# The beginning of a fused RWKV attention and mixture-of-experts kernel: decay logarithms earlier, the bonus as two operations over all heads, identity products on TensorE

## What is computed

```python
x = x + attn(layernorm(x))      # 16 heads of 16 channels
x = x + moe(layernorm(x))       # 8 experts, top 2, capacity 320 per batch row
```

```python
Wmat = where(i > j, w ** (i - j - 1), 0) + eye * u     # w = exp(-exp(time_decay))
y    = (r @ k * Wmat) @ v + r @ state * w ** i
out  = (groupnorm(y) * ln_w + ln_b) * gelu(g) @ Wo.T
```

## Time and profile before

| | us |
|---|---|
| median of 3 runs | 866.69 |
| lowest, highest | 865.9, 867.45 |
| the profiled execution | 867.18 |
| its span in the profile | 865.1 |
| TensorE matmuls busy | 826.1 (95% of the span) |
| VectorE busy | 498.3 (58%) |
| ScalarE busy | 490.9 (57%) |
| GpSimd busy | 465.3 (54%) |

### The profile page before, as it was taken

How to read it: one execution, slowest core, us unless ns; L and a number is a source line. 1 busy time by engine, 2 the same in 40 slices (tenths; PEclk the granted TensorE clock), 3 DMA queues, 4 the chain that set the end, 5 groups by cost and what they waited for, 6 DMA issues and landing times. The chain is left out here.

```text
span 865.1 us, 17505 instructions
## 1 busy us (share of the span) xinstructions
PE 826.1 (95%) x6343; PEld 679.8 (79%) x6343; DVE 498.3 (58%) x1237; ACT 490.9 (57%) x876; POOL 465.3 (54%) x497
## 2 busy tenths in 40 slices
PE   3999999999999997999999999999999999999995
PEld 3678878778878776878898787898788888787884
DVE  6888888998888755435442543443543543443441
ACT  4578888888888795445533534543543543552331
POOL 6455477777787765575435455435355443436214
PEclk9999999999999999999999999999999999999998
DMA  4942131113111122754234334334145242404113
GB/s 147 357 174 69 39 129 53 51 51 102 58 50 52 52 85 70 217 138 124 69 49 82 99 73 83 97 69 88 57 104 93 70 97 31 115 2 50 19 13 42
DMA packets 50471, 74.01 MB, mean 86 GB/s; under 512 B 5056, under 2 KB 42176, under 8 KB 50368
## 3 DMA queue, kind: packets, MB, share of 16 engines
q1 hardware_dynamic: 35488, 53.46, 18.9%
q0 software_dynamic: 14592, 19.18, 13.0%
q10 hardware_dynamic: 288, 0.01, 0.0%
HBM read 38.41 MB, written 34.22 MB: 84 GB/s over the span
## 5 line engine op out<-in xcount | busy, mean ns | idle before, releaser
L1584 POOL DMA_INDIRECT out<-ysb,index x80 | 124.7, 1559 | 146.3 <-DVE ysb L1820 110.1
L1933 PE MATMUL p<-xh,whi 128*128 128x512 f32 (+1 forms) x504 | 190.1, 377 | 4.6 <-PEq L1486 4.0
L1797 DVE TENSOR_TENSOR hid<-gated,p 128x512 f32<-128x512 f32 (+1 forms) x126 | 80.9, 642 | 193.9 <-ACT gated L1646 193.9
L1935 PE MATMUL p<-xh,wlo 128*128 128x512 f32 (+1 forms) x504 | 189.9, 377 | 0.0
L1934 PE MATMUL p<-xl,whi 128*128 128x512 f32 (+1 forms) x504 | 189.6, 376 | 0.0
L1646 ACT ACTIVATE gated<-p 128x512 f32<-128x512 f32 (+1 forms) x126 | 70.9, 563 | 174.8 <-PE p L1935 174.8
L1959 PE MATMUL py<-w,hh 128*128 128x512 f32 x448 | 162.4, 403 | 3.7 <-DVE hl L1081 3.0
L1573 POOL TENSOR_TENSOR wlo<-wraw,whi 128x448 fp32r<-128x448 f32 x56 | 71.2, 1274 | 97.8 <-ACT whi L1632 93.7
L1933 PEld LDWEIGHTS p<-xh,whi 128*128 128x128 f32 x504 | 94.7, 188 | 25.7 <-issue 7.4
L1934 PEld LDWEIGHTS p<-xl,whi 128*128 128x128 f32 x504 | 95.0, 188 | 18.7
L1935 PEld LDWEIGHTS p<-xh,wlo 128*128 128x128 f32 x504 | 94.7, 188 | 18.6
(11 more groups left out here) (204 smaller groups left out, 1440.1 us busy)
## 6 DMA issues: line engine op xcount, KB each, us to landing
wraw<-in_w SPq DMA_DIRECT2D x24, 896.0 KB, 5.0
disp<-wraw SPq DMA_DIRECT2D x16, 662.5 KB, 9.2
xtok<-disp SPq DMA_DIRECT2D x16, 530.0 KB, 5.5
x_ring<-in_x SPq DMA_DIRECT2D x16, 256.0 KB, 4.0
out<-x SPq DMA_DIRECT2D x16, 256.0 KB, 2.2
xtok<-disp SPq DMA_DIRECT2D x8, 265.0 KB, 4.0
out<-ysb,index POOLq DMA_INDIRECT x80, 3.8
disp<-row,slot_i POOLq DMA_INDIRECT x64, 2.9
```

What stands on the lines that cost most here:

```text
L1584: nc.gpsimd.indirect_dma_start(out, bass.IndirectOffsetOnAxis(ap=index[e.const % 2][:, t:t + 1], axis=0), ysb[j % NY][:], None, compute_op ...
L1797: nc.vector.tensor_tensor(hid[k][:, 0:w], gated[k][:, 0:w], p3[k][:, 0:w], ALU.mult).then_inc(hid_ready, 1)
L1933: nc.tensor.matmul(dst[:, 0:w], hi[m][:, wcut], xh[xcut], start=(kt == 0), stop=False)
L1935: ins = nc.tensor.matmul(dst[:, 0:w], lo[m][:, wcut], xh[xcut], start=False, stop=(kt == KT - 1))
```

## The change

Four edits, all in the program's beginning:

1. `decay_logs` moves on DVE from iteration c = -1 (behind `mixing(0, 1)`) to iteration c = -3, behind `stats1(0)`. Its exponential on ACT moves from behind `pairs(0)` to behind `turned1(0)`, and `decay_tables` from behind `key(0)` to in front of `receptance(0)`.
2. `stats1(2)` moves on DVE from in front of `mixing(0, 2)` to behind the four masks of step 0.
3. `bonus` becomes two operations over all heads: identity times u into a borrowed tile (`kept.xtok`), and `dmask` plus that tile. The first stands in front of `decayed_k(0)`, the second behind it.
4. PE issues 14 products of the identity with itself in front of `turn1(0)` and 6 behind it. They write into `pY`, which nobody reads before the first `across`, a product that starts a new sum there.

```diff
+BEFORE_TURN, BEHIND_TURN = 14, 6
...
             turned1(c + 1)
+            if c == -1:
+                mask_table()
             group_rstd(c - 1)
...
             normed2(c - 2)
+            if c == -1:
+                decay_tables()
             receptance(c + 1)
             pairs(c + 1)
-            if c == -1:
-                mask_table()
             key(c + 1)
-            if c == -1:
-                decay_tables()
...
+        on_diagonal = kept.xtok[:].rearrange("p t c -> p (t c)")[:, 0:H * Q].rearrange("p (h q) -> p h q", q=Q)
-        def bonus(half):
+        def bonus():
             dve.wait_ge(late_in, 16 * NLATE)
+            chain.link(nc.vector.tensor_tensor(on_diagonal, ident[:].unsqueeze(1).to_broadcast([P, H, Q]),
+                                               u_sb[:].unsqueeze(2).to_broadcast([P, H, Q]), ALU.mult))
+        def add_bonus():
             dve.wait_ge(set_act, 2)
-            for h in range(half * H // 2, (half + 1) * H // 2):
-                ins = nc.vector.scalar_tensor_tensor(dmask[:, h, :], ident[:], u_sb[:, h:h + 1], dmask[:, h, :],
-                                                     ALU.mult, ALU.add)
-            chain.link(ins)
+            chain.link(nc.vector.tensor_tensor(dmask[:], dmask[:], on_diagonal, ALU.add))
...
             if c == -1:
-                decay_logs()
                 head_parity()
...
-            stats1(c + 3)
+            if c != -1:
+                stats1(c + 3)
+            if c == -3:
+                decay_logs()
...
             if c == -1:
-                bonus(0)
+                bonus()
             decayed_k(c + 1)
             if c == -1:
-                bonus(1)
+                add_bonus()
...
             if c == -1:
+                stats1(2)
                 slot_tables()
...
+        def warm(n):
+            for _ in range(n):
+                nc.tensor.matmul(pY[:, 0, 0:P], ident[:], ident[:], start=True, stop=True)
         for c in range(-1, TAIL):
+            if c == -1:
+                warm(BEFORE_TURN)
             scores_a(c)
             across(c, 0)
             turn1(c + 1)
+            if c == -1:
+                warm(BEHIND_TURN)
```

## The result

The change made the kernel slower: 872.72 us (median; 871.91 to 873.47) against 866.96 (865.90 to 867.45), a ratio of 1.0065 [1.0049, 1.0081], 5.8 us. The forecast was 866.1 with a range up to 867.4.

What follows compares the result with a forecast made beforehand. TensorE was taken to bound the kernel, through step 1's first projection. Masks 1.55 us earlier less 1.0 for moved statistics gave 0.55 gained: 866.6 for the profiled execution, 866.1 for the median, range 863.2 to 867.4.

Steps and rivals of the forecast that it cites:

- What bounds the kernel: TensorE has least room, so each edit is measured by the start of step 1's first projection, 30.18 us before.
- Edit 1: Logarithms in VectorE's first pause hold POOL's second norm operation; `shift` comes 1.9 us later (bounds 0 to 2.3).
- Edit 4: Early identity products, hidden in TensorE's waits, may raise its clock, winning 0.43 us at transposes and 1.42 at first projection.
- The sum up to v: Centring of v's weight ends at 17.2 instead of 19.38, so v's projection starts 2.3 us earlier than 19.53.
- Edits 3 and 2: Two-operation bonus worth nothing by itself on VectorE, masks 1.55 us earlier; moved statistics cost 1.0 us behind the masks.
- v to masks: Step 0, from the start of v's projection at 17.2 to the masks' start at 23.8.
- the second rival: POOL's two operations precede the bonus product; step 1's projection at 30.4, 0.2 us late; 867.2, bad case 868; chance 0.15.
- Masks to start: First projection of step 1 comes 5.8 us behind the masks, including 1.0 for the moved statistics.
- The first (no hold): Rival: POOL's first norm isn't held, step 1's first projection at 27.0, gain 3.2 us, 863.5; chance 0.24.
- the 0.08 for slower: Chance of a time above 868.4 us: the second rival's far end and what had not been seen.

Runs made afterwards that it cites:

- e1: The kernel before plus only the 20 identity products (14 ahead of the first transposes, 6 behind); 871.80 us, ratio 1.0055.
- e5: The kernel before plus the 20 identity products cut to one column each, so the array has next to nothing to do; 872.15 us, ratio 1.0056.
- e13: The kernel before plus 80 already fulfilled waits on TensorE spread over iterations 1 to 10, no products; 870.54 us, ratio 1.0043.
- e12: The kernel before plus the 20 identity products and 177 already fulfilled waits spread over TensorE's attention iterations; 868.73 us, ratio 1.0020.
- e15: The whole changed kernel plus 177 already fulfilled waits spread over TensorE's iterations 1 to 12; 866.84 us, ratio 0.9995.
- e6: The kernel before plus seven full identity products ahead of the first transposes and none behind; 869.51 us, ratio 1.0022.
- e10: The kernel of e7 plus four 512-column products, three ahead of the first transposes and one behind; 866.26 us, ratio 0.9989.
- e2: The changed kernel without the identity products, the other three edits kept; 867.33 us, ratio 1.0002.
- e4: The kernel before plus only the early decay logarithms; 866.49 us, ratio 0.9995.
- e7: The kernel before plus the early decay logarithms, with VectorE waiting for step 0's first `rstd` ahead of them; 865.39 us, ratio 0.9979.
- e16: The whole changed kernel plus the 177 spread waits and VectorE's wait for the first `rstd` ahead of the logarithms; 865.26 us, ratio 0.9970.
- e3: The changed kernel with the decay logarithms and their exponentials back in the old places; 870.85 us, ratio 1.0043.
- e14: The kernel of e7 plus the 20 identity products and 177 already fulfilled waits on TensorE; 865.37 us, ratio 0.9978.
- e11: The kernel of e7 plus the bonus as two operations over all heads; 865.21 us, ratio 0.9974.
- e9: The kernel before plus 80 already fulfilled waits at the beginning of TensorE's stream; 875.64 us, ratio 1.0101.

## Why the prediction was wrong

**What bounds the kernel: here is the step that failed.** "The measure of the change is therefore one instant: the start of the first projection of step 1". That the rest of the program stays the same was assumed with it, and the products were priced by their duration alone. But their number moved the expert phase by 79 instructions in TensorE's stream, and 3 to 4 us of pauses came between 440 and 740 us (e1, e5, e13 have them, e12 and e15 have not). The waits of the kernel before had a small sign of it, the 0.6 us at `py` behind a join, but no row that gives the price of moving it; the question to ask was what a longer stream does to the branches behind it. The start itself failed as well: it was forecast at 29.6 and came at 32.55. Of these 3.0 us, 2.2 were the clock (32.55 against e15's 30.37); the rest is the hold at the centring, less what was regained behind it (both below).

The Trainium skill has a rule that I didn't weigh ("Runtime: NRT & Kernel Launch", Instruction fetch mechanics): instructions are fetched in blocks of 256 in sequence, and a taken branch whose target lies outside the fetched window stalls its engine. The runs agree with the size (moved by 79 the pauses come, moved by 256 they go) and with the place (where TensorE leaves the arm of an If). The trace agrees further in that each of the 27 pauses ends 1.2 to 1.7 us behind the end of a 16 KB packet of instructions. What TensorE does in those last 1.2 to 1.7 us no record shows, and packets stand at joins without a pause too, so that this is the mechanism fits well and isn't proven. e6 and e10, moved by 28 and 16 or one less, had one pause, ahead of or among the third join's transposes, and not the one that before has 2 us further on.

**Edit 1: right.** Held 1.9 us: `var` took 2.12 where 0.23 was, in after, e2, e4 and e15 alike; the transposes were forecast at 10.1 and came at 10.01. e7 shows its price from the other side, a start 1.6 us earlier than e4's (28.17 and 29.79) and 1.4 in the time by the ratios (0.9979 against 0.9995 of e4).

**Edit 4: half right.** "If the products bring the upper level forward": in e1, e15 and e16 transposes and first projection ran at it, in after the transposes did not. What wasn't foreseen is that the level can fall again, and the granted clock of 0.50 shows it: at v in after (3.65), e3 (3.50), e1 (2.89) and e12 (2.85), in the first projection of e14 (2.52). In e15 and e16 it stayed up. Little came of it even there: e14 has v at 18.04 and e7 at 18.03, and the same time; e16 has v at 16.96 and the masks at 22.39, 1.0 us ahead of e7, but its start only 0.2 ahead, and a time that can't be told from e7's.

**The sum up to v: one hold was missed.** The centring was forecast to end at 17.2. In e15, where the clock did what was forecast, it ended at 19.19, since `vmean` took 1.73 us beside POOL's `r_dec` and MEMSET. The earlier v of that sum (2.3 us) became 0.2.

**Edits 3 and 2: near in size.** v to masks was forecast as 17.2 to 23.8, 6.6 us. In e15 it was 19.34 to 24.76, 5.4: POOL had done its two operations (`r_dec` at 16.02) ahead of the bonus product, as the second rival had it, but beside the centring, where they delayed `vmean` and not the product. In e2 and e16 the order was the forecast's: the product came first, and `r_dec` took 3.18 and 3.31 us for 1.27. On the time itself edit 3 was forecast at nothing, and e11 against e7 is 0.2 us. Masks to start: 5.8 forecast, 5.6 measured. So the start came at 30.37 where 29.6 was forecast: v 2.14 later (1.55 of it `vmean`'s hold), 1.18 and 0.19 regained behind it. That e15's 866.84 lies inside the forecast's range is in part luck: a hold that was missed and a stretch that was priced too long nearly cancel.

**The rivals.** The first (no hold) fell. The second had the right sign and a wrong mechanism (and a slip: 0.2 us late from the median of 866.7 is 866.9 and not 867.2). None of the three spoke of the program behind 31 us; the 0.08 for slower had no mechanism but the second rival's far end and "what I have not seen".

## What to carry to other kernels

Instructions that are added to an engine with branches later on cost more than their time: look for new pauses marked "issue" where it leaves a branch, and for a packet of instructions in the DMA view that ends shortly ahead of them, and shift the stream by some harmless instructions before you believe that an edit is bad (or good). Where VectorE has a long operation with two inputs in SBUF, put it behind the small POOL operations that others wait for, by a wait if need be: that wait was worth 1.4 us to edit 1 (e7 against e4) and 2.2 to the whole change in its other place (e16 against e15), which without it can't be told from no change (e15). An edit in the first 30 us is to be judged with its stream length held the same.

## What the runs showed of the hardware

- 80 instructions that do nothing, in a stream of thousands, cost 3.7 us (e13); 177 more beside 79 give 3.0 back (e12 against e1). A pause is up to 1.95 us (e5). Each of the 27 ends 1.2 to 1.7 us behind a 16 KB packet of instructions that took 0.9 to 1.4 us; e3, with the same stream as after, has only two of the three.
- VectorE's TENSOR_SCALAR of 128 x 32, with one tensor input, took 1.5 us more beside POOL's `r_dec` and MEMSET and ended within 0.03 us of the MEMSET's end (after, e15; 0.18 in the kernel before and in e2).
- TensorE's level isn't set by the stream alone: the same first 30 us gave transposes of 1.11 and 0.66 us in after and in e15. After's were preceded by 2.36 us idle and e15's by 1.53, since its products had run longer. The idle alone doesn't set it either: v took 3.65 behind 2.33 us idle in after and 1.96 behind 2.30 in e15. Whether this goes with the execution or the chip stays open; only one profile of each was taken.
- The granted clock read 1.00 over the first projection of the kernel before, which took 3.41 us and not 1.99, but 0.50 over the slow v of after: a reading of 1.00 doesn't rule out the lower level, the durations decide.
- An instruction with two fulfilled waits isn't free in front of waiting work: 80 of them at the beginning (e9) moved the transposes from 8.20 to 11.24.
